# A graph layer with routed experts: the f16 copy of GELU moved ahead of the signs, the registers of a node tile read at the head of its end

## What is computed

```python
xn = _layernorm(x)
# graph attention: a softmax over the edges of each source node
Wh = xn @ W_w + W_b
e = (Wh @ a_w[:256])[dst] + (Wh @ a_w[256:])[src] + a_b[0]
e = where(e > 0, e, 0.2 * e)
ex = exp(e - segment_max(e, src)[src])
att = ex / segment_sum(ex, src)[src]
h = relu(segment_sum(att[:, None] * Wh[dst], src))
# linear attention over all nodes, 8 heads: elu + 1 on queries and keys, projection
x = x + h + linear_attention(xn)
# experts: top 2 of 8, each gelu(x @ w1 + b1) @ w2 + b2
x = x + moe(_layernorm(x))
```

## Time and profile before

| what | us |
|---|---|
| median of 3 runs | 2242.29 (2235.94 to 2250.9) |
| the profiled execution | 2250.89 |
| its span, first to last instruction | 2249.1 |
| VectorE (DVE) busy | 1676.1, 75% |
| TensorE (PE) busy | 1711.7, 76% |
| ScalarE (ACT) busy | 963.0, 43% |
| GpSimd (POOL) busy | 985.1, 44% |
| mean granted TensorE clock | 0.888 of full speed |

### The profile page before, as it was taken

How to read it: one execution, slowest core, us unless ns; L and a number is a source line. 1 busy time by engine, 2 the same in 40 slices (tenths; PEclk the granted TensorE clock), 3 DMA queues, 4 the chain that set the end, 5 groups by cost and what they waited for, 6 DMA issues and landing times.

```text
span 2249.1 us, 40227 instructions
## 1 busy us (share of the span) xinstructions
PE 1711.7 (76%) x13588; PEld 1261.0 (56%) x13588; DVE 1676.1 (75%) x4219; ACT 963.0 (43%) x2291; POOL 985.1 (44%) x988
## 2 busy tenths in 40 slices
PE   3778875641887578888856888887878788889998
PEld 2557562531765466666634555655555555566666
DVE  5999898652666667786667888888788878875665
ACT  6322130211332232222224656565656566656555
POOL 3000003325666666665666666665666656610000
PEclk7899997875999788888877999999999999989999
DMA  5011120113655344433333333333332334930000
GB/s 171 18 55 61 43 72 22 55 44 89 174 162 156 100 124 118 108 101 93 88 83 89 84 91 86 93 84 91 79 93 79 93 78 90 81 40 10 11 20 12
DMA packets 121460, 182.21 MB, mean 81 GB/s; under 512 B 21490, under 2 KB 91902, under 8 KB 121214
## 3 DMA queue, kind: packets, MB, share of 16 engines
q0 software_dynamic: 45312, 120.06, 23.0%
q1 hardware_dynamic: 75904, 59.25, 8.4%
HBM read 152.43 MB, written 26.63 MB: 80 GB/s over the span
## 4 chain that ended last, share of the span: by engine, by line
DVE 41%; PE 25%; issue 17%; another core or an unknown queue 8%; ACT 5%; DVEq 2%; POOL 1%; ACTq 0%; DMA 0%; SPq 0%; POOLq 0%
PE bank L1215 6%; PE bank L1231 5%; DVE mloc L1561 4%; DVE big L1478 3%; DVE scr L1583 3%; DVE big L1745 3%; DVE big L1483 3%; DVE big L1480 2%; DVE work L1758 2%; DVE big L1485 2%; DVE scr L1443 2%; DVE work L1539 2%; DVE work L1556 1%; PE bank L1049 1%
## 5 line engine op out<-in xcount | busy, mean ns | idle before, releaser
L640 POOL DMA_INDIRECT work<-table,tiles x904 | 911.9, 1009 | 573.9 <-PE bank L1083 299.5
L1231 PE MATMUL bank<-big 128*128 128x256 f16 x2352 | 329.9, 281 | 24.5 <-issue 23.2
L1081 PE MATMUL bank<-work,scr 128*128 128x257 f16 x904 | 270.0, 299 | 24.3 <-issue 14.2
L1215 PE MATMUL bank<-scr,big 128*128 128x512 f16 (+1 forms) x1248 | 277.0, 371 | 0.6 <-ACT big L843 0.3
L1082 PE MATMUL bank<-work,scr 128*128 128x256 f16 x904 | 270.6, 299 | 7.0 <-issue 6.6
L1231 PEld LDWEIGHTS bank<-big 128*128 128x128 f16 x2352 | 235.4, 100 | 67.0 <-issue 31.3
L1083 PE MATMUL bank<-work,scr 128*128 128x257 f16 x904 | 268.7, 297 | 3.7 <-issue 3.5
L1583 DVE SCALAR_TENSOR_TENSOR scr<-scr,gg,bank 128x257 f32<-128x257 f32 x452 | 216.6, 479 | 51.3 <-remote 19.1
L762 ACT ACTIVATE work<-bank 128x1024 f16<-128x1024 f16 x113 | 115.7, 1024 | 310.6 <-DVE mloc L1561 211.3
L972 PE MATMUL bank<-big 128*128 128x208 f16 x1568 | 176.9, 268 | 73.1 <-DVE big L1485 54.8
L972 PEld LDWEIGHTS bank<-big 128*128 128x128 f16 x1568 | 150.5, 102 | 99.4 <-issue 94.1
(11 more groups left out here) (342 smaller groups left out, 3416.6 us busy)
## 6 DMA issues: line engine op xcount, KB each, us to landing
work<-table,tiles POOLq DMA_INDIRECT x904
scr<-normed_cols SPq DMA_DIRECT2D x98, 128.0 KB
table<-big SPq DMA_DIRECT2D x49, 129.0 KB, 2.2
normed_rows<-scr SPq DMA_DIRECT2D x49, 128.5 KB, 2.8
big<-normed_rows SPq DMA_DIRECT2D x49, 128.5 KB
normed_cols<-big SPq DMA_DIRECT2D x49, 128.0 KB, 1.7
xs<-in_x_dram SPq DMA_DIRECT2D x4, 1536.0 KB, 14.5
out_dram<-work SPq DMA_DIRECT2D x48, 128.0 KB
```

Of the source, the lines that this page charges most:

```text
L640: pool.indirect_dma_start(G[:, r, j, :], None, table, bass.IndirectOffsetOnAxis(ap=col[:, t:t + 1], axis=0)).then_inc(rows_in[r // GS], 16)
L1081: pe.matmul(of[:, 0:D + 1], hi, Gh[:, r, j, 0:D + 1], start=(j == 0), stop=False)
L1215: mm = pe.matmul(bank[5 + f][:, 0:n * P], w1p[pw][:, e, h, f * P:(f + 1) * P], x2p[b % 2][px][:, h, 0:n * P], start=(h + m == 0), stop=(h ...
L1231: mm = pe.matmul(of, hTp[ph][:, k % 2, f, (j + c) * P:(j + c + 1) * P], w2p[pw][:, e, f, :], start=False, stop=(f == 1 and m == 2))
```

## The change

Two parts. On ACT, in a step with an expert, the f16 copy (`hidden_hi`) is called right behind the GELU, ahead of the Sign, where it was called behind the Sign and the one-column Exp. On VectorE, `window_end` reads its registers at the head of its block, behind the memset and ahead of `dn`, and no longer waits for its own add into `xs`. `wid` is now that of the tile which ends, where it was loaded for the next one; `last_group` is the next tile's as before. The wait on `f_x` stands at the head of the block for the adds of earlier tiles (a memset at the start raises `f_x` by one, so that the first block's wait is met), and `windows_added` waits for all adds so far in `mixed` and `norm_stats`.

```diff
                 if s in UP_AT:
                     hidden(*UP_AT[s])
+                    hidden_hi(*UP_AT[s])
                 if s + 2 < NS:
                     one_hot_turned(s + 2)
                     if s in UP_AT:
                         act.activation(ready[:, s:s + 1], epsc[:, :], ACT.Exp)
-                if s in UP_AT:
-                    hidden_hi(*UP_AT[s])
...
-            dve.reg_load(wid, wids[0:1, 0:1])
             dve.reg_mov(window, 0)
             dve.reg_load(last_group, tendi[0:1, 0:1])
             link(dve.memset(U, 0.0))
             link(dve.memset(mx[:, 1, GS:GS + 1], 0.0))
+            dve.memset(started[:, 3:4], 0.0).then_inc(f_x, 1)
...
                 with dve.If(dve.snap(last_group) == g + 1):
                     w = dve.snap(window, min_val=0, max_val=W - 1)
+                    pause()
+                    dve.reg_load(wid, wids[0:1, ds(w, 1)])
+                    dve.reg_load(last_group, tendi[0:1, ds(w + 1, 1)])
+                    dve.wait_ge(f_x, w + 1)
                     dve.wait_ge(e_U, g + 1)
                     dve.tensor_scalar(dn[:, :], U[:, D:D + 1], 1e-30, None, ALU.max).then_inc(f_dn, 1)
...
                     dve.tensor_tensor(x_w, x_w, hh, ALU.add).then_inc(f_x, 1)
-                    dve.wait_ge(f_x, w + 1)
-                    pause()
-                    dve.reg_load(last_group, tendi[0:1, ds(w + 1, 1)])
-                    dve.reg_load(wid, wids[0:1, ds(w + 1, 1)])
                     dve.reg_add(window, window, 1)
+
+            def windows_added():
+
+                dve.wait_ge(f_x, dve.snap(window, min_val=0, max_val=W) + 1)
...
             def mixed(p):
...
+                windows_added()
                 dve.wait_ge(a_pj, p + 1)
...
             def norm_stats(b):
                 n = of_batch[b]
+                windows_added()
                 for j in range(n):
```

## The result

In the comparison that the forecast was made for, the changed kernel takes 2234.14 us (median of 22 runs) and the kernel before 2243.55 (22 runs). The ratio is 0.9953, 95% interval 0.9936 to 0.9971: by the ratio 10.5 us, or 0.5%, faster (the medians are 9.4 apart). One of the changed kernel's 22 runs took 5308.69 us, and the ratio leaves it out. The forecast was 2217, 25 us less than the runs shown then. The time lies in the range given (2196 to 2244) and outside the forecast's own range (2205 to 2228); the time of the first rival, TensorE absorbs it, was 2232.

What follows compares the result with a forecast made beforehand. VectorE's chain was taken to bound the third stage, with TensorE close (busy 668 and 651 of 803 us). Register and copy terms sum to 30.6 us, less 5.6 for TensorE: 2242 - 25 = 2217 us, own range 2205 to 2228, full range 2196 to 2244.

Steps and rivals of the forecast that it cites:

- the first rival: TensorE's waits ahead of the scores grow as VectorE gets earlier; some 10 of 25 us remain, 2232 us; chance 0.22.
- worked out 0.57 and 1.18: Tile ends: dn's delay in us after its update starts, for tiles ending on the first and second update of a pair.
- The second rival: Register loads run only after the memset, so 0.9 us moves ahead of dn; 9.5 us remain, 2233 us; chance 0.15.
- 16.6 + 3 + 1.5 - 1.5: Register part: gains in third, second and first stages, less 1.5 us for new f_x waits in mixed and norm_stats.
- The share of the first stage, +1.5: Register gain in the first stage, 540 to 1002 us: only 5 of 16 tiles, of the second kind, win 1.5 us.
- the 14 of 21: Third stage: of 21.2 us the split waits for the f16 copy, 14 us counted as won, bounds 8 and 21.
- charged with 3: Copy delays the Sign in 21 of 61 steps; 7 that TensorE ends charged 0.45 us each, 3 us lost (0 to 16).
- I take off 5.6 for that: Deduction of 5.6 us from 30.6 because the shortest steps, 10.6 us, become bound by TensorE's 10.5 us a step.
- the 20 steps: Third-stage steps whose scores wait for TensorE's signal, 18.1 us in all; there VectorE's gains ahead of them are lost.
- a wait above 25 us: Check in the third stage: the scores' wait for TensorE was to be not above 25 us.
- The sum of 30.6 uncapped: All terms before the TensorE deduction: 16.6 + 3 + 1.5 + 14 - 1.5 - 3 = 30.6 us.
- The third rival: Copy holds the Sign in nearly every step, delaying spread and TensorE's loop: 28 us slower, 2270 us; chance 0.08.

Runs made afterwards that it cites:

- a full TensorE: Second product of both halves written twice (28 more matmuls in 104 steps): kernel before 2195.95 us, changed 2179.89, copy alone 2194.10, registers alone 2178.48; plain kernel before 2063.42.

## Why the prediction was wrong

**The registers: right in price and in place.** dn comes 0.59 and 1.21 us after its update (worked out 0.57 and 1.18), and the stop of 0.95 us behind the add is gone. The second rival, loads that wait for the memset, is out: its sign, 1.4 us ahead of every dn, is not there. The sum of 16.6 + 3 + 1.5 - 1.5 = 19.6 us stands beside 24.8 on a chip where TensorE is not late and 17.5 with a full TensorE. On the first kind it is only an estimate, the difference of the two ratios: some 13 us, each ratio good to about 5, about half of the 24.8. The share of the first stage, +1.5, isn't seen in the profiles of the second kind: that stage takes 386.3 us before, 387.8 with the registers alone and 389.5 with both parts. There dn stands 1.2 us or more behind its update in all 16 tiles, and why nothing is left of the 0.3 us a tile is open. The prediction also prices one stop twice, at 1.04 us for a tile that ends on the first of a pair and at 0.95 for one that ends on the second; that is 1 us of its sum.

**The copy ahead of the signs: right in mechanism, wrong in what it is worth.** The stops went, all of them (23.8 to 2.1 us), and not the 14 of 21 that I counted; where TensorE is not late the copy is worth 19.5 us, with no sign of a price for the late Sign (charged with 3). On a chip like that of the forecast it is worth 0.0, interval 5 less to 6 more.

**The step that failed** is the one of TensorE as the last: "I take off 5.6 for that". It had to be about 20: 30.6 - 5.6 = 25 was forecast, 10.5 measured. I worked out TensorE's need from its busy time, 10.5 us a step, and took the 20 steps whose scores wait for it as the only ones it ends. But its signals come 3.2 us after the recorded ends. Already before the change 30 of 60 steps of the third stage have scores that start with the signal, some of them without a wait to show for it, and VectorE has only to get ahead for more steps to end so: the scores wait in 29 steps after the change, with 20.0 us more of waiting. The prediction had named the sign for this, a wait above 25 us, and it is 38.1. The first rival had this mechanism and its price (2232 against 2234 measured); it got 0.22 because the ends of tiles fall in other steps than the 20. That argument counts which steps TensorE ends before the change, and the change moves them.

Why the copy's part goes whole and not the registers' can be read from the distance between the spread's recorded end and the scores, third stage, second kind of chip. Its median is 3.0 us before and with the registers alone, 2.6 with the copy alone and 2.4 with both, and its lower quartile 3.0, 3.0, 2.0 and 2.0. The copy's stops stand behind the spread, and taking them out uses up the time that a signal 3.2 us late needs. Of the tile ends of the third stage at most one stands straight ahead of the scores (in the first stage 15 of 16 do), and with the registers alone the spread moves along with VectorE. The experiments show which part goes (copy alone 0.0 and 1.9 us); that the place of the stop is the reason is my reading of these distances and wasn't tried by itself.

**The sum of 30.6 uncapped** was too low for a chip on which TensorE is in time: 43 and 44 us were measured there. The difference is 8.5 us in the copy's part (19.5 against 14 - 3) and 5 in the registers'. So on the first kind of chip the gain lost to TensorE is over 30 us, not 20, if the parts are worth as much there.

**The third rival** fell. The copy ahead of the Sign is better by 9.4 us than the copy behind it, on the second kind of chip.

**Left open**: why TensorE's signals are late on one kind of chip. A full TensorE divides the gain in a similar way, but in the third stage it is busy 97% of the time (753 of 777 us) and on the first kind 83% (664.98 of 803), so it is a stand-in and not the cause. Nor was the registers' part measured by itself on the first kind.

Of the versions run that leave nothing out, none beats the changed kernel; on the first kind of chip only the copy alone was run beside it.

## What to carry to other kernels

A wait in the profile of one core that is put down to "remote" can be a signal that comes later than the record of the work that raises it, as here; measure that lateness from the semaphore's increments, and add it to the engine's chain before deciding which engine ends a step. A stop that stands straight ahead of a meeting of two engines is, by this case, worth only the other engine's slack there, whatever its length. And a sum of stops holds for a kernel on one chip: the same change gave 10 us and 43 us on two kinds of chip, with nothing in the program set otherwise.

## What the runs showed of the hardware

- The same program takes 2243 us in the first comparison and on one chip of the experiments, and 2062 to 2067 on four others, 8% less, with a mean granted clock of TensorE of 0.888 and 0.933 in the profiles of the kernel before. The page of the second kind:

```profile
span 2058.0 us, 40227 instructions
## 1 busy us (share of the span) xinstructions
PE 1634.1 (79%) x13588; PEld 1228.5 (60%) x13588; DVE 1669.9 (81%) x4219; ACT 963.7 (47%) x2291; POOL 1008.5 (49%) x988
```

VectorE's work is the same to 0.4% (1676.1 us on the first kind); what differs is how long it waits.

- Leaving out 904 of TensorE's 13588 matmuls made the kernel before 5.5 us slower (1.0016 to 1.0037). From 485 to 640 us the granted clock is 0.82 with them left out and 0.89 in a kernel that has them, on the same chip (the copy alone):

```profile
485.00:640.00 155.00, 117.54 (x776) 96.57 (x777) 97.59 (x242) 49.56 (x135) 108.54 (x111) 0.82 0.59 168
```
```profile
485.00:640.00 155.00, 121.06 (x885) 101.62 (x886) 102.50 (x254) 52.16 (x144) 113.35 (x114) 0.89 0.62 175
```

TensorE with less to do was at the higher of its two levels (1.2 and 2.4 GHz) for less of that stretch. That this is the reason for the 5.5 us was not tried by itself. In the third stage leaving them out changes nothing in VectorE's busy time or in the pace of the steps (737 us for its last 60 steps, 738 in the kernel before).

- A register load of VectorE from SBUF takes 0.31 us in the median (149 of them in the kernel before, 0.30 to 0.32 for nine in ten) and runs beside a vector instruction: two loads in a row behind the first update of a pair leave dn at 0.59 us in place of 0.52. The Trainium skill, page "DMA: Bandwidth & Descriptors", section "Latency and other measured facts", gives a tensor_load a floor of about 600 ns; this case doesn't agree.
